# Both attentions of an eight-layer kernel: factors ahead of the values' layout, loads with an outermost dimension of 8 or 16, and in the second one ScalarE copies a quad's sums

## What is computed

```python
# first attention (L0)
Q = (x @ Wq.T).reshape(H, b, s, dkh)      # also K, V: heads by a plain reshape
scores = jnp.einsum('hbqd,hbkd->hbqk', Q, K)
out = jnp.einsum('hbqk,hbkd->hbqd', jax.nn.softmax(scores, axis=-1), V).reshape(b, s, -1)
y = out + x
return (y - mu) / jnp.sqrt(var + EPS)     # over each batch of x

# second attention (L3)
q, k, v = heads of x @ Wqkv.T + bqkv
q, k = _apply_rope(q, cos, sin), _apply_rope(k, cos, sin)
attn = softmax(einsum('bhqd,bhkd->bhqk', q, k) / sqrt(HEAD_DIM))
return (attn @ v) @ Wout.T + bout
```

## Time and profile before

| | |
|---|---|
| median of 3 runs | 2195.09 us (2167.61 to 2204.93) |
| profiled execution | 2174.91 us |
| its span | 2173.2 us |
| mean granted TensorE clock | 0.730 |
| PE busy | 1710.9 us (79%) |
| DVE busy | 1243.8 us (57%) |
| ACT busy | 1013.9 us (47%) |
| POOL busy | 706.9 us (33%) |

### The profile page before, as it was taken

The page is one execution under the profiler, slowest core; times in us unless marked ns, Lnnn a source line. Parts: engine busy times, 40 slices in busy tenths (PEclk is TensorE's granted clock), DMA queues, the critical chain, the costliest instruction groups (busy, mean ns, idle before and its releaser), DMA issues. The chain is left out here.

```text
span 2173.2 us, 25740 instructions
## 1 busy us (share of the span) xinstructions
PE 1710.9 (79%) x8437; PEld 897.6 (41%) x8437; DVE 1243.8 (57%) x2968; ACT 1013.9 (47%) x2001; POOL 706.9 (33%) x1320
## 2 busy tenths in 40 slices
PE   2889889989963598573762693299999998889998
PEld 1333233333312477562662462133333333367776
DVE  3655555556946655503666752487677778545543
ACT  2344444545745234224662421165555666745453
POOL 2422223222215345606634385233123320012211
PEclk8555555556965766585665797577577889989999
DMA  4111111111100300010004123211111111010000
GB/s 117 52 44 44 42 38 42 43 45 43 44 1 1 98 1 10 8 40 15 3 1 139 38 41 58 71 48 45 37 59 50 58 52 45 17 41 11 7 9 15
DMA packets 90785, 85.54 MB, mean 39 GB/s; under 512 B 41053, under 2 KB 70791, under 8 KB 90523
## 3 DMA queue, kind: packets, MB, share of 16 engines
q1 hardware_dynamic: 79794, 75.63, 10.9%
q0 software_dynamic: 7680, 6.06, 1.7%
q10 hardware_dynamic: 3176, 2.20, 0.3%
HBM read 55.56 MB, written 29.36 MB: 39 GB/s over the span
## 5 line engine op out<-in xcount | busy, mean ns | idle before, releaser
L980 DVE TENSOR_REDUCE arena<-psum 128x2 f32<-128x1024 f32 x512 | 615.0, 1220 | 347.4 <-PE psum L772 345.2
L886 ACT ACTIVATE arena<-psum 128x512 f32<-128x512 f32 x1024 | 546.0, 597 | 354.5 <-PE psum L787 351.1
L787 PE MATMUL psum<-pairs 35*128 35x512 f32 x1024 | 500.3, 583 | 70.3 <-ACT arena L886 53.6
L772 PE MATMUL psum<-pairs 33*128 33x512 f32 x1024 | 504.1, 590 | 62.0 <-DMA pairs<-arena 35.5
L787 PEld LDWEIGHTS psum<-pairs 35*128 35x128 f32 x1024 | 217.3, 244 | 519.3 <-ACT arena L886 295.2
L797 PE MATMUL psum<-arena 128*32 128x512 f32 x2048 | 383.0, 831 | 1.5 <-ACT arena L886 1.5
L772 PEld LDWEIGHTS psum<-pairs 33*128 33x128 f32 x1024 | 219.1, 248 | 96.9 <-DVE arena L980 36.8
L679 POOL TENSOR_TENSOR arena<-arena 128x16 fp32r<-128x16 f32 x64 | 14.1, 221 | 588.6 <-DVE arena L980 588.6
L2500 POOL TENSOR_SCALAR arena<-arena 128x4 f32<-128x4 f32 x112 | 30.2, 270 | 437.4 <-DVE arena L2494 431.5
L2529 ACT ACTIVATE arena<-arena 128x128 f32<-128x128 f32 x216 | 88.6, 481 | 139.5 <-POOL arena L2506 119.6
L2677 ACT ACTIVATE arena<-psum,arena 128x512 f32<-128x512 f32 x128 | 85.7, 684 | 84.9 <-PE psum L2618 82.1
(11 more groups left out here) (432 smaller groups left out, 2418.3 us busy)
## 6 DMA issues: line engine op xcount, KB each, us to landing
L_q_parts<-arena SPq DMA_DIRECT2D x32, 256.0 KB, 8.4
L_k_parts<-arena SPq DMA_DIRECT2D x32, 256.0 KB, 9.7
arena<-L_q_parts SPq DMA_DIRECT2D x64, 128.0 KB
pairs<-L_q_parts SPq DMA_DIRECT2D x64, 128.0 KB
arena<-L_k_parts SPq DMA_DIRECT2D x120, 64.0 KB
pairs<-L_k_parts SPq DMA_DIRECT2D x120, 64.0 KB
arena<-in_L_ffn_w SPq DMA_DIRECT2D x1, 2048.0 KB, 10.8
ec_result<-arena SPq DMA_DIRECT2D x1, 2048.0 KB, 9.8
```

The lines of the kernel that those rows point to most:

```text
L772: last = nc.tensor.matmul(maxes.bank(("max", i, m))[:, 512 * n:512 * n + 512], columns(q9, MAX_ROW, i, g, 128 * (first + n), 128), columns ...
L787: nc.tensor.matmul(acts.bank(name), columns(k9, ROWS, i, g, 128 * k, 128), columns(q9, ROWS, i, g, 0, 512), start=True, stop=True).then_in ...
L886: nc.scalar.activation(prob[:, k % 2, g, :], acts.bank(name), ACT.Exp, scale=scale).then_inc(act_taken, 1)
L980: nc.vector.tensor_reduce(neg_max[:, i % 2, 4 * g + first:4 * g + first + 2], maxes.bank(("max", i, m)).rearrange("p (h t) -> p h t", h=2) ...
```

## The change

Five edits, all in `attention_layer` and the functions inside it:

- Queries are loaded by two DMAs a half, one for each copy, with (d, part) as rows: outermost dimension 8 of 2 rows of 4 KB. Keys are loaded by one DMA a half, 16 (part, d) rows with each doubled: outermost dimension 16. A half's rows are now (copy, d, part) for the queries and (part, d, copy) for the keys.
- `of_x.factors(pool, b + 1)` goes from r = 3, after `lay_values`, to r = 2, after the operands.
- `x_spread` goes from (2, 2) to (2, 0) on VectorE.
- In the second attention ScalarE does the copy of `out_bank`, after the exponentials of k = 0 of the next quad; VectorE's copy goes.
- In the second attention SP stores a batch's parts at r = 2 and 3, not 1 and 2.

```diff
--- before.py
+++ after.py
@@ -524,17 +524,18 @@
 
         return slice(LANES * h + PRODUCTS, LANES * h + LANES)
 
-    def query_rows(i, h):
-
-        rows = q_parts[i // TPB, i % TPB, h].rearrange("a d t -> (a d) t")
-        return rows.unsqueeze(0).to_broadcast([PARTS, PARTS * HD, 1024])
-
-    def load_keys_of(eng, i, h, k_to):
+    def load_queries_of(eng, i, h, q_to):
 
         for a in range(PARTS):
             at = LANES * h + PARTS * HD * a
-            rows = k_parts[i // TPB, i % TPB, h, a].unsqueeze(0).to_broadcast([PARTS, HD, 1024])
-            eng.dma_start(k_to[at:at + PARTS * HD, :], rows).then_inc(qk_in[i % RING], 16)
+            rows = q_parts[i // TPB, i % TPB, h].rearrange("a d t -> d a t")
+            eng.dma_start(q_to[at:at + PARTS * HD, :], rows).then_inc(qk_in[i % RING], 16)
+
+    def load_keys_of(eng, i, h, k_to):
+
+        rows = k_parts[i // TPB, i % TPB, h].rearrange("a d t -> (a d) t")
+        eng.dma_start(k_to[LANES * h:LANES * h + PRODUCTS, :],
+                      rows.unsqueeze(1).to_broadcast([PARTS * HD, PARTS, 1024])).then_inc(qk_in[i % RING], 16)
 
     def put_max_rows(eng, i):
 
@@ -585,8 +586,7 @@
                         sp.wait_ge(act_made, acts.count(("score", i - RING, 3, 3)))
                     q_to, k_to = q_words[:, i % RING, :], k_words[:, i % RING, :]
                 for h in range(HALVES):
-                    at = slice(LANES * h, LANES * h + PRODUCTS)
-                    sp.dma_start(q_to[at, :], query_rows(i, h)).then_inc(qk_in[i % RING], 16)
+                    load_queries_of(sp, i, h, q_to)
                     if keys:
                         load_keys_of(sp, i, h, k_to)
 
@@ -613,8 +613,8 @@
                 if i < LAST:
                     max_rows(i + 1)
                 r, b = i % TPB, i // TPB + AHEAD
-                if rope and r in (1, 2) and b < B:
-                    store(b, r - 1)
+                if rope and r >= 2 and b < B:
+                    store(b, r - 2)
                 if i + RING < QUADS:
                     load(i + RING)
                 if by_tokens and b < B:
@@ -719,10 +719,10 @@
                     operand(b, r)
                 if rope and r in (1, 2) and b < B:
                     operand(b, r - 1)
+                if r == 2 and b + 1 < B:
+                    of_x.factors(pool, b + 1)
                 if r == 3 and b < B:
                     lay_values(b)
-                if r == 3 and b + 1 < B:
-                    of_x.factors(pool, b + 1)
                 if i + 2 < QUADS:
                     split_max(i + 2)
                 if by_tokens and i + RING < QUADS:
@@ -889,6 +889,13 @@
                 act.wait_ge(act_made, acts.count(("turn", i)))
                 nc.scalar.activation(max_row[0:MAXES, i % 2, :], acts.bank(("turn", i))[0:MAXES, 0:128], ACT.Copy).then_inc(act_taken, 1)
 
+            def out(i):
+
+                act.wait_ge(pv_step, 4 * i + 4)
+                if i >= 2:
+                    act.wait_ge(o_done, i - 1)
+                nc.scalar.activation(o_quad[:, i % 2, :], out_bank, ACT.Copy).then_inc(out_taken, 1)
+
             def load_keys(i):
 
                 act.wait_ge(stored[slot_of(0, 1)], 16 * PARTS)
@@ -919,6 +926,8 @@
                 b = i // TPB + AHEAD
                 for k in range(4):
                     exps(i, k)
+                    if rope and k == 0 and i >= 1:
+                        out(i - 1)
                     if k == 0 and i < LAST:
                         rows(i + 1)
                     if b + 1 < B and i % TPB == 3:
@@ -931,6 +940,8 @@
                         keep(b, 1)
                     if b < B and (i % TPB, k) == (2, 3):
                         keep_values(b)
+            if rope:
+                out(LAST)
 
         @block.vector
         def _(dve):
@@ -985,11 +996,7 @@
                 dve.wait_ge(pv_step, 4 * i + 4)
                 if i >= 2:
                     dve.wait_ge(o_done, i - 1)
-                if by_tokens:
-
-                    nc.vector.transpose(o_quad[:, i % 2, :], out_bank).then_inc(out_taken, 1)
-                else:
-                    nc.vector.tensor_copy(o_quad[:, i % 2, :], out_bank).then_inc(out_taken, 1)
+                nc.vector.transpose(o_quad[:, i % 2, :], out_bank).then_inc(out_taken, 1)
 
             def normalise(i):
 
@@ -1043,7 +1050,7 @@
                 for k in range(4):
                     if i + 2 < QUADS:
                         take(i + 2, 2 * k)
-                    if k == 0 and i >= 1:
+                    if by_tokens and k == 0 and i >= 1:
                         out(i - 1)
                     if i + 2 < QUADS:
                         take(i + 2, 2 * k + 1)
@@ -1057,9 +1064,10 @@
                         o_spread(b)
                     if rope and b < B and (r, k) == (1, 2):
                         add(b)
-                    if b < B and (r, k) == (2, 2):
+                    if b < B and (r, k) == (2, 0):
                         x_spread(b)
-            out(LAST)
+            if by_tokens:
+                out(LAST)
             normalise(LAST)
```

## The result

The changed kernel takes 1923.6 us (median of 4 runs, 1904.8 to 1940.1) beside 2188.9 for the kernel before (2167.6 to 2204.9). The ratio is 0.875, 95% interval 0.861 to 0.888. The prediction was 1935 (1885 to 2065). On another chip the same kernel took 1942.2 beside 2223.5, ratio 0.877 (0.870 to 0.883). Runs of one kernel spread by 1 to 6% with the clock that they were granted, so a ratio with an interval is of the fast runs alone, and times and the other ratios are of the medians of all runs.

What follows compares the result with a forecast made beforehand. A stall at r = 3 was taken to drop TensorE's clock; at the high clock TensorE, ScalarE and VectorE share the limit. Terms -14 - 152 - 14 - 2 - 70 - 7 = -259 gave 1916, plus 19: 1935 us (1885 to 2065).

Steps and rivals of the forecast that it cites:

- The clock as the main term: Quads 3 to 22: without the r = 3 stall the clock stays high, -152 us in the first attention, -70 in the second.
- (a): Operand loads spread over more DMA engines: -14 us in each attention's prologue, and waits for maxima's rows go.
- R4: Rival: the new loads stay slow, losing the prologues' 28 and some 12 us of waits; near 1975 us; chance 0.03.
- The main case: Whole kernel: the clock stays high and the loads get fast, 1885 to 1985 us; chance 0.50.
- (b): Factors ahead of `lay_values`, `x_spread` at (2, 0): ScalarE's 6.4 and 2.8 us waits go at no cost; direct gain 28 and 10 us.
- The 19 us put on for falls: Whole kernel: allowance for two or three remaining clock falls and the median lying above the profile, added to 1916 us.
- (c): Second attention, ScalarE copies the sums: per fast quad VectorE 11.0 to 10.3 us, ScalarE 9.8 to 10.4; cost taken as 0.
- (d): Second attention, rotary operands stored one quad later: SP no longer waits for POOL, 25 us in total; counted as nothing.
- R1: Rival: the clock still falls about once a batch, at r = 2, k = 0; half the clock gain stays, 2031 us; chance 0.24.
- R2: Rival: in both attentions the falls have another cause than the stalls; 2097 us (2070 to 2150); chance 0.09.
- R2b: Rival: falls have another cause in the second attention alone, -70 shrinks to -10 there; 1976 us; chance 0.07.
- R3: Rival: ScalarE's copy holds up TensorE and the whole second attention runs at 1.2 GHz; slower by 43 us or more; chance 0.03.

Runs made afterwards that it cites:

- factors_late: The changed kernel with the factors back at r = 3 after `lay_values` and `x_spread` back at (2, 2): 2119.4 us, ratio 0.964 to the kernel before.
- the doses: Two variants of the changed kernel, factors at r = 3 ahead of `lay_values` behind varying numbers of idle POOL memsets: 2006.4 and 2067.3 us beside 2202.9.
- loads_only: The kernel before with the new loads and nothing else: 2150.1 us beside 2197.5, ratio 0.978.
- factors_only: The kernel before with only the factors moved to r = 2 and `x_spread` to (2, 0): 2115.8 us, ratio 0.963.
- vector_again: The changed kernel with VectorE copying the sums in the second attention, a repeat on another chip: 1933.7 us, ratio 0.870.
- after_again: The changed kernel, unchanged, run again on another chip: 1942.2 us, ratio 0.877 to the kernel before.
- half_exps: The changed kernel with exponentials of only 256 of 512 columns: 1953.9 us beside 2202.9 for the kernel before.

## Why the prediction was right, point by point

- **The clock as the main term: right.** Stall of r = 3, fall, 4.07 for 2.66 us a block (from one block's products to the next). -155.4 for -152 and -66.2 for -70. Shown by `factors_late`, by the doses, and by `loads_only`, in which the stall stays and the clock falls.
- **(a) Prologues: right in size.** -14.0 for -14 in the first. In the second, from the issue of the first queries to TensorE's first matmul 30.0 us became 17.0 (TensorE starts at 1203.10 after SP's first issue at 1186.07), -13 for -14; some 3 us of it were lost between the attentions, which I don't explain.
- **(a) as cover: wrong.** R4 priced slow loads at "near 1975": the prologues and 12 us of waits. `factors_only`, which is that case without the copy's move and the later stores, took 2115.8. The rows that say so stood there: 10.7 us of load in a quad of 11.1, POOL's in-order wait at the regrouping, and two falls of the clock behind waits for maxima's rows, which R4 priced at their length alone. I priced the loads against the slow quad's slack when the change made the quad fast. The main case didn't rest on this, because the loads did get fast.
- **(b) at no cost: right.** POOL's wait in r = 2 covered the factors; ScalarE's wait is gone.
- **(b), quads 0 to 2: left out.** 19 us came from the clock rising at 71 us, at the first projections, not only at the first values. That varies: in `vector_again` and `factors_late` the clock rose late (first quads of 21.7, 16.8 and 18 us), in `loads_only` and `after_again` early. No run ties it to an edit of this change, so in this profile it is luck as far as is known. The second attention varies too: in `after_again` the clock was high from quad 4 on only, and its quads 0 to 22 took 332.7 us for 301.8, which is 31 of the 45 us between the two profiled executions.
- **The 19 us put on for falls: not in the profile, but in other runs.** The profiled execution had no fall in either loop before quad 30; `after_again` lost 31 us by the late rise and one fall. At 1904.8 us the profiled execution lies 11 under the sum of 1916; without the early rise it would lie 8 above.
- **(c): the mis-sized term.** Foretold 11.6 us for an empty quad of the second attention, measured 12.3 (-1.9 us for -7 in its quads 23 to 29), and 52.0 for 51 a batch. VectorE's and ScalarE's sums of 10.3 and 10.4 are no bound if the two engines take turns with TensorE. The move is worth nothing measurable, where the wait for maxima's rows was what the old 12.6 had in it.
- **(d) at nothing: open.** No run has the later stores alone.
- **Rivals.** R1 did not come about in the first profile. TensorE idles 0.5 us at (2, 0), not the 1.5 us that R1 was built on. Its mechanism is real: one fall in `after_again`, two in ten with VectorE's copy, three in five where the idle was 1.2 us (`half_exps`, first attention). But a fall there cost 4 us in the kernel after, not half the gain. R2 and R2b fell with the doses. R3 did not appear: TensorE's wait for the copy shows twice in the whole second attention, 0.7 and 0.6 us.

## What to carry to other kernels

Where TensorE's granted clock has two levels in a loop, find the idle in front of each fall before anything else; here moving four small instructions a quad ahead was worth about 190 us. Then ask what the faster loop needs: a transfer that hides in the slow loop may be the bound of the fast one, and two edits that bring 2% and 4% alone can bring 12% together. And a high busy share names a bound only if halving that engine's work shortens the loop.

## What the runs showed of the hardware

- TensorE's clock fell from 2.4 to 1.2 GHz at idles of 0.92 to 4.60 us at r = 3, 16 of 16 times in the dose kernels; I had expected the border between 1.2 and 2 us. Elsewhere a fall came only sometimes: waits for a DMA of 1.0 to 1.5 us two times in nine (kernel before), of 0.8 to 1.6 us six times in eight (`factors_only`), and idles of 0.49 and 0.91 us at (2, 0) 3 times in 18 and 2 in 10.
- Once at 1.2 GHz a stretch can stay there with TensorE busy in every record: 83.8 of 83.8 us in the tail of `factors_only`, while the same quads in the kernel after run at 2.4 GHz throughout. Inside the loops the clock rose only in quads r = 0 and r = 2, which have the 128-row projections, and not in every one of them; the tail has none.
- A load whose outermost dimension is a broadcast of 2 moved at 49 GB/s. With outermost dimensions of 8 and 16 the same 512 KB came in some 4 us, with up to 160 GB/s in a window.
